# The head-output copy on ScalarE instead of VectorE, and another spread of a pair's stage work over its 32 steps

## The reference

```
mod = (silu(c) @ wmod)            # six rows per batch: sa, ca, ga, sb, cb, gb
h = layernorm(x) * (1 + ca) + sa
q, k, v = split(h @ W_pack)       # 16 q heads, 8 k and 8 v heads of 128
q, k = rope(q), rope(k)
k, v = conv2(k, w_k), conv2(v, w_v)      # two taps along the rows
p = softmax(mask(q k^T / sqrt(128)))     # causal, window of 128
x = x + ga * ((p v) @ W_o)
h = layernorm(x) * (1 + cb) + sb
xn = rmsnorm(h) * w_norm          # the router and the experts read xn
# router: softmax over 32 experts, top 4, at most 128 rows per expert
# expert and shared expert: (silu(xn Wg) * (xn Wu)) Wd, the shared one gated
x = x + gb * (h + experts + shared)
```

## Time and profile before

| what | value |
|---|---|
| median of 3 runs | 818.39 us (815.42 to 822.55) |
| the profiled execution | 815.22 us, of which the span of its instructions is 813.0 |
| TensorE busy | 754.8 us (93%) |
| VectorE busy | 544.1 us (67%), 1692 instructions |
| ScalarE busy | 458.0 us (56%), 1148 instructions |
| GpSimd busy | 427.4 us (53%) |
| granted TensorE clock, mean over the span | 0.985 |

### The profile page before, as it was taken

How to read it: one execution, slowest core, us unless ns; L and a number is a source line. 1 busy time by engine, 2 the same in 40 slices (tenths; PEclk the granted TensorE clock), 3 DMA queues, 4 the chain that set the end, 5 groups by cost and what they waited for, 6 DMA issues and landing times.

```text
span 813.0 us, 12301 instructions
## 1 busy us (share of the span) xinstructions
PE 754.8 (93%) x3858; PEld 621.3 (76%) x3858; DVE 544.1 (67%) x1692; ACT 458.0 (56%) x1148; POOL 427.4 (53%) x337
## 2 busy tenths in 40 slices
PE   4878999999999999899999999999889799998997
PEld 2567888887788888778888878888667567776774
DVE  4578776678877768888686786878454115554265
ACT  4667777777787576778676768776352112221110
POOL 0533435554366388645548855655703605675475
PEclk9999999999999999999999999999898989999999
DMA  8943900000004111100401002040368438997671
GB/s 305 306 100 95 341 1 1 2 0 2 1 1 135 48 38 45 38 1 0 155 2 52 36 21 72 2 156 10 107 173 244 123 110 225 296 296 164 151 250 52
DMA packets 62351, 84.45 MB, mean 104 GB/s; under 512 B 6312, under 2 KB 50229, under 8 KB 62288
## 3 DMA queue, kind: packets, MB, share of 16 engines
q1 hardware_dynamic: 53456, 74.04, 29.0%
q0 software_dynamic: 7680, 8.95, 5.5%
q10 hardware_dynamic: 1152, 0.69, 0.3%
HBM read 54.88 MB, written 33.51 MB: 109 GB/s over the span
## 4 chain that ended last, share of the span: by engine, by line
PE 69%; DVE 14%; ACT 8%; issue 5%; another core or an unknown queue 2%; DMA 2%; SPq 0%; POOL 0%; ACTq 0%; DVEq 0%; POOLq 0%
PE PJ L1269 17%; PE OUT L1367 10%; PE U L1356 5%; PE U L1322 5%; PE U L1518 5%; PE U L1345 4%; PE U L1460 3%; PE OUT L1460 3%; PE U L1321 3%; PE U L1357 3%; ACT U L536 2%; PE U L1269 2%; PE XB L1537 2%; PE OUT L1537 2%
## 5 line engine op out<-in xcount | busy, mean ns | idle before, releaser
L731 POOL TENSOR_TENSOR qsw<-qsw,sinT 128x512 f32<-128x512 f32 x96 | 123.7, 1288 | 222.4 <-ACT qsw L523 221.8
L536 ACT ACTIVATE U<-U,nmax 128x128 f32<-128x128 f32 (+1 forms) x256 | 99.1, 387 | 86.7 <-DVE nmax L928 81.5
L928 DVE CUSTOM_DVE_ANT_0 U<-U,mask 128x128 f32<-128x128 f32 (+1 forms) x256 | 86.8, 380 | 74.7 <-PE U L1322 74.4
L1367 PE MATMUL OUT<-wo,oT 128*128 128x256 f32 x512 | 133.3, 384 | 0.0
L1269 PE MATMUL PJ<-hT_hi,w_hi 128*128 128x512 f32 x256 | 112.1, 438 | 0.8 <-issue 0.8
L1269 PE MATMUL PJ<-hT_lo,w_hi 128*128 128x512 f32 x256 | 101.0, 395 | 0.0
L1269 PE MATMUL PJ<-hT_hi,w_lo 128*128 128x512 f32 x256 | 100.9, 394 | 0.0
L735 POOL TENSOR_TENSOR qr<-qr,qsw 128x512 f32<-128x512 f32 x64 | 82.4, 1288 | 30.0 <-DVE qr L916 26.7
L938 DVE TENSOR_SCALAR prob<-U,rinv 128x128 f32<-128x128 f32 (+1 forms) x256 | 95.1, 413 | 4.5
L1367 PEld LDWEIGHTS OUT<-wo,oT 128*128 128x128 f32 x512 | 88.7, 193 | 6.9
L522 ACT ACTIVATE qsw<-PJ 64x512 f32<-64x512 f32 x96 | 57.0, 593 | 63.3 <-PE PJ L1269 57.8
(11 more groups left out here) (202 smaller groups left out, 1596.9 us busy)
## 6 DMA issues: line engine op xcount, KB each, us to landing
wgu<-in_dram SPq DMA_DIRECT2D x32, 352.0 KB
expert_sum<-blank SPq DMA_DIRECT2D x3, 2176.0 KB, 17.3
wd<-in_dram SPq DMA_DIRECT2D x16, 352.0 KB
slot_rows<-blank SPq DMA_DIRECT2D x1, 4624.0 KB, 24.7
xe<-slot_rows SPq DMA_DIRECT2D x16, 289.0 KB, 4.6
late_sums<-expert_sum SPq DMA_DIRECT2D x9, 512.0 KB, 9.8
wraw<-in_dram SPq DMA_DIRECT2D x8, 512.0 KB, 13.3
bcm<-mod_rows SPq DMA_DIRECT2D x8, 512.0 KB, 6.7
```

The costliest lines, as they stand in the source:

```text
L536: last = act.activation(U[n % 3][:, a:z], U[n % 3][:, a:z], ACT.Exp, scale=-1.0, bias=nmax[:, n % 4, j:j + 1], accum_out=rsum[:, n % 4, j: ...
L731: pool.tensor_tensor(pair3(qsw[:, n % NQSW, :]), pair3(qsw[:, n % NQSW, :]), both(sinT[:, :]), ALU.mult).then_inc(t2_done, 1)
L928: last = dve.tensor_tensor_reduce(out=U[n % 3][:, a:z], in0=U[n % 3][:, a:z], in1=mask[:, a:z], scale=-float(HD) ** -0.5, scalar=3.4e38, o ...
L1367: last = pe.matmul(OUT[b][:, t * H:(t + 1) * H], oT[:, n % NOT, t * PN:(t + 1) * PN], wo[:, head, :], start=(head == 0 and t == 0), stop=( ...
```

## The change

The copy of a head's output moves from VectorE to ScalarE, where it stands between the projection copies and the exponentials of a step. The tables of the hooks change: on ScalarE the square roots of prepare_norm and post_std go from step 5 to 6, and the squares from 7 and 8 to 10 and 12; on VectorE the next pair's statistics go from steps 0 and 3 to steps 28 and 30 of the pair before that (for the second pair, to steps 3 and 5 of the first), its norm from 8 and 9 to 7 and 8, its low parts from 16 and 19 to 20 and 25, the second half of post_stats from step 4 to 5, post_h2 from 6 and 7 to 9 and 11, keys and carry from 25 to 26; on GpSimd the first scatter goes from step 26 to 27.

```diff
--- before.py
+++ after.py
@@ -543,6 +543,10 @@
                     act.wait_ge(pv_ps, n - 1)
                 act.activation(pT[:, n % 2, :], U[n % 3][:, 0:3 * PN], ACT.Copy).then_inc(pt_done, 1)
 
+            def head_out(n):
+                act.wait_ge(pv_ps, n + 1)
+                act.activation(oT[:, n % NOT, :], U[n % 3][:, 0:S], ACT.Copy).then_inc(ot_done, 1)
+
             def v_rows(G):
                 act.wait_ge(vt_ps, G + 1)
                 if G >= 2:
@@ -590,7 +594,7 @@
                 q, _ = next_step(n)
                 if n < 0 or n >= NU:
                     return
-                if l == 5:
+                if l == 6:
                     if q < NPAIR:
                         prepare_norm(q)
                     if p >= 0:
@@ -601,8 +605,8 @@
                     if l in (13, 15):
                         prepare_hi(q, (l - 13) // 2)
                 if p >= 0:
-                    if l in (7, 8):
-                        post_squares(p, l - 7)
+                    if l in (10, 12):
+                        post_squares(p, (l - 10) // 2)
                     if l == 12:
                         post_rms(p)
                     if l in (14, 17):
@@ -638,6 +642,8 @@
                     v_rows(n // 4)
                 if 0 <= n + 3 < NU:
                     project(n + 3)
+                if 0 <= n - 2 < NU:
+                    head_out(n - 2)
                 if 0 <= n < NU:
                     exps_of(n)
                 if 0 <= n - 1 < NU:
@@ -761,7 +767,7 @@
                 pool.tensor_tensor(h, h, xres[:, 2 * b:2 * b + 2, :], ALU.add).then_inc(base_done, 1)
 
 
-            FIRST_SCATTER = 26
+            FIRST_SCATTER = 27
             SCATTERS = {}
             at, c = FIRST_SCATTER, 0
             while c < TT * TOPK:
@@ -937,10 +943,6 @@
                 for j, (a, z) in enumerate(((0, PN), (PN, 3 * PN))):
                     last = dve.tensor_scalar(prob[:, n % 2, a:z], U[n % 3][:, a:z], rinv[:, n % 4, j:j + 1], None, ALU.mult)
                 last.then_inc(norm_done, 1)
-
-            def head_out(n):
-                dve.wait_ge(pv_ps, n + 1)
-                dve.tensor_copy(oT[:, n % NOT, :], U[n % 3][:, 0:S]).then_inc(ot_done, 1)
 
             def w_low(n):
 
@@ -1083,21 +1085,23 @@
             def hooks(n):
                 p, l = post_step(n)
                 q, _ = next_step(n)
+
+                if q == 1 and l in (3, 5):
+                    prepare_stats(q, (l - 3) // 2)
+                if q + 1 < NPAIR and l in (28, 30):
+                    prepare_stats(q + 1, (l - 28) // 2)
                 if q < NPAIR:
-                    if l in (0, 3):
-                        prepare_stats(q, l // 3)
-                    if l in (8, 9):
-                        prepare_norm(q, l - 8)
-                    if l in (16, 19):
-                        prepare_lo(q, (l - 16) // 3)
+                    if l in (7, 8):
+                        prepare_norm(q, l - 7)
+                    if l in (20, 25):
+                        prepare_lo(q, (l - 20) // 5)
                 if p >= 0:
                     if l in (1, 2):
                         post_gate(p, l - 1)
-                    if l == 4:
-                        post_stats(p, 0)
-                        post_stats(p, 1)
-                    if l in (6, 7):
-                        post_h2(p, l - 6)
+                    if l in (4, 5):
+                        post_stats(p, l - 4)
+                    if l in (9, 11):
+                        post_h2(p, (l - 9) // 2)
                     if l in (13, 14):
                         post_xn(p, l - 13)
                     if l in (15, 18):
@@ -1110,7 +1114,7 @@
                         post_slots(p)
                     if l == 24:
                         post_probs(p)
-                    if l == 25:
+                    if l == 26:
                         post_keys(p)
                         post_carry(p)
                 if p == LAST - 1 and l in (16, 19, 20, 28):
@@ -1136,8 +1140,6 @@
             for n in STEPS:
                 if 0 <= n < NU:
                     scores(n)
-                if 0 <= n - 2 < NU:
-                    head_out(n - 2)
                 if 0 <= n + 3 < NU:
                     project(n + 3)
                 if n % 4 == 3 and n + 1 < NU:
```

## The result

The changed kernel takes 824.31 us (median of 20 runs, 817.9 to 833.5); the kernel before, in 20 runs beside it, 818.22 us (814.96 to 823.24). The ratio is 1.0067, with a 95% interval of 1.0045 to 1.0089: 5.5 us slower, give or take 1.8. A ratio leaves out executions that ran over 1.5% above the fastest of their kernel (two of these twenty; three of the twelve in the run with post_h2 sooner), so it is not quite the quotient of the medians, which are 6.1 us apart here. The forecast of 817 us lies on the other side of no change. The profiled execution took 824.49 us, 822.4 of them span.

The account below looks back on a forecast made before the run. TensorE's own work bounds most steps; where it waits, ScalarE's late exponentials and VectorE's queue do. Terms -9.2 + 7.2 + 1.0 + 1.9 + 0.9 = +1.8 on the profiled 815.2 us gave 817; range 806 to 827.

Parts of the forecast that it names:

- The base: Whole kernel: the sum of +1.8 us was added to the profiled execution's 815.2; the median shown, 818.4, lay 3.2 above it.
- The bound and the gain of 9.2: Steps 6 to 8, pairs 1 to 3: ScalarE's late exponentials and VectorE's queue stall TensorE; the moved tables gain 9.2 us.
- The head copies: All 128 steps: each copy costs ScalarE 0.30 us start to start (0.25 to 0.48), with nothing gained or lost in plain steps.
- Steps 10 to 14: Pairs 1 to 3: ScalarE's queue makes the copy T(12) of transposed probabilities 2.7 us late; 7.2 us lost in all.
- step 15's wait of 0.9: Step 15: a stall of about 0.9 us whose causes the change leaves untouched, so it was left out of the sum.
- The clock: Behind the new wait at step 14: half a fall to half rate, 0.9 us lost; ends 0 and 5.1.
- The first pair: Pair 0: statistics move to step 5 and the table pair to step 6; 1.0 us lost, ends 1.5 gained and 4.5 lost.
- the silu's 1.9: Tail: the last head copy stands ahead of the first silu's table load, so VectorE's product starts 1.9 us later; ends 0 and 2.4.
- The unnamed wait of the earlier trace: Before the last steps: ScalarE's 3.17 us "remote" wait at 585.44 may go (811 to 814) or a new one cost as much; chance 0.07.
- What was called free: Low parts, keys, carry and scatters one to six steps later, statistics a pair ahead: hidden by TensorE's pace, no cost.
- The rival in which ScalarE becomes the bound: Slower exponentials and copies: steps 6 to 14 lose 1.4 + 5 per pair, pair 0 4.5, tail 1.9; about 825 us; chance 0.17.

## Why the prediction was wrong, point by point

- **The base: the step that turned the sign.** The sum said +1.8, slower, which is the way it went. It was put on the profiled execution's 815.2, an execution 3.2 us faster than the median of its kernel, and so came out as 817, below that median. The forecast named those 3.2 us and left them out; on the median it would have been 820.2. Of the 7.3 us from 817 to 824.31, 3.0 are this base (818.22 - 815.2), and 4.3 are terms, mis-sized as told below.
- **The bound and the gain of 9.2: right.** Steps 7 to 10 gave back 3.4 us (20.49 to 17.05), 3.9 (20.94 to 17.03) and 2.2 (18.75 to 16.51): 9.6. At step 8 about 0.6 remains (0.5 forecast).
- **The head copies: right.** 0.39 each alone, 0.28 from the copy to the exponentials behind it (0.30 taken), nothing gained or lost in plain steps; the copy alone gave a ratio of 0.9981. ScalarE's busy time rose by 34 us, not the 45 to 50 of the forecast: 128 copies of 0.39 are 50, but each overlaps its follower by 0.1.
- **Steps 10 to 14: right in place, the sum within 0.5.** T(12) was to be 2.7 late. TensorE waits 0.31, 0.92 and 1.69 in steps 13 and 14: 2.9. Steps 13 to 16 without a fall of the clock lose 2.7 to 2.8 (2.5 and 2.2 forecast). That the sum is so near is in part luck, since two terms in it were off and met: post_h2 in step 11 took 2.9 us (222.22 to 225.15), not 1.91; and step 15's wait of 0.9, which I left, shrank to 0.3 to 0.4 where the clock held. My reading that the head copies tip it was wrong: without them it is as long. The 2.9 could have been read before: the 1.91 of the earlier trace rows is the first half of post_h2, and the second half's last two instructions took 1.90, not 0.88, in the trace of the kernel before as well:

```profile
199.82 0.88 DVE L987 SCALAR_TENSOR_TENSOR h<-h,std,bcm 128x256 f32<-128x256 f32 x2
...
204.82 1.90 DVE L987 SCALAR_TENSOR_TENSOR h<-h,std,bcm 128x256 f32<-128x256 f32 x2
```
- **The clock: the term that was mis-sized.** I took 0.9 for half a fall. There is one in the second and one in the third pair, every time: 1.3 us net in step 14 (4.0 lost in steps 13 to 16, where 2.7 are lost without it) or 1.6 in steps 21 and 22, so 2.5 to 3.3 in all. I looked for a fall behind a wait only; the one in steps 21 and 22 comes with no wait at all, behind the logits, and the kernel before, with its longer waits in steps 7 to 10, has none in these pairs. Why it has none is open.
- **The first pair: mis-sized.** 1.0 forecast, 2.3 to 2.7 found against before, 3.1 against the run with its tables as before. I counted that the table pair moves beside a k tap and a high half, and not what it moves away from: the wait of 4.5 us ahead of the exponentials of step 6 that had hidden it.
- **The tail: the silu's 1.9 was right, the wait ahead of it was not priced.** From 602.85 to 604.77 there are 1.9 us of load and silu, as forecast. The unnamed wait of the earlier trace rows, to which I gave 0.07, grew from 3.1 us behind the transposes to 6.7 (5.2 in the second profile). I had called the scatters' later start free because GpSimd has time; they run beside ScalarE's last copies. That the later start makes the wait longer is not shown: ScalarE's idle time ahead of this copy was 3.1 to 3.2 us in the four profiles with scatters from step 26 that nothing holds back, and 1.6 to 5.2 in the seven with such scatters from step 27.
- **What was called free and was:** statistics a pair ahead, low parts, keys and carry: no wait of TensorE names them (in the loop GpSimd's scatters wait 1.3 us at most for the keys).
- **A sum that does not come out.** The rival in which ScalarE becomes the bound adds 3 x 2.4 + 4.5 + 1.9 to 815.2, which is 829 and not about 825, so above the range of 806 to 827.

With the measured terms the sum is -9.6 + 8.1 + 2.5 + 2.7 + 5.6 = +9.3 in the first profiles, where the span grew by 9.4, and -9.6 + 8.1 + 2.9 + 2.3 + 3.2 = +6.9 in the second, where it grew by 9.0; there the rest is in stages that vary (+4.8 at the end, -2.9 in the routing, +1.5 in step 0, -1.4 ahead of the first scores). The runs give +5.5 give or take 1.8, so the sums of single profiles are at its upper end or above. The +1.8 of the forecast misses by the first pair (1.3 to 1.7), the clock (1.6 to 2.0) and the tail (1.3 to 3.7). The rule that speaks of a drain behind a table load (the Trainium skill, ScalarE: Activation LUTs, What ACT_TABLE_LOAD costs) does not show here either: the load at 231.65 ends at 232.93 and the next instruction starts at 232.95.

## What to carry to other kernels

Before a table load, a root or any fixed cost is moved, find the wait in which it passes now: moved out of it, it is paid in full, and the empty wait gives nothing back. Time taken out of a TensorE-bound stretch may come back as half clock, so read the granted clock of the whole pair, not only behind the waits. A forecast that adds a difference to one execution inherits how far that execution lies from the median: add it to the median. A run of indirect DMAs that an idle engine "can do at any time" belongs away from the last steps of a chain, or into two short runs.

## What was not expected of the hardware

ScalarE started late beside long runs of GpSimd's scatters. Where 13 or 14 ran one behind the other next to steps 125 to 127, a copy or head copy of ScalarE started up to 5.2 us after the matmuls that it waits for and the instruction before it had ended (2.0 to 5.2 at the longest of each profile), in all eleven such profiles, from about the eighth scatter on; with none beside it, or six or seven in a row, none did. What in the chip makes it is open: the trace says "remote".

The clock fell from 2.4 to 1.2 GHz in stretches in which TensorE was busy for 4.00 of 4.00 us. The Trainium skill (TensorE: Matmul & The Clock Gate, Part 1) has the half rate as the state after idling and the full rate as that of activity; these stretches hold no idling that the profile shows (busy 4.00 of 4.00, then 0.57). No run here settles whether the rule and the rows fit: just ahead of each of these falls stand the 24 matmuls of 34 columns, and the kernel before runs the same in step 21 of each later pair and stays at 1.00.

VectorE's second pass of post_h2 took 1.90 us instead of 0.88 where a product of GpSimd (1.27 us from 223.68) ran beside it. In the loops of the 17 profiles 49 instructions of post_h2 took 1.4 to 1.6 us, each beside a product of GpSimd that had started between 0.41 us before it and 0.04 after it; the other 359 took 0.71 at most.
